# P V turned round in the attention of a fused audio tower, and the slot table emptied during the first attention

## The reference, cut to what matters

```python
content = einsum('bhld,bhmd->bhlm', q + u_bias, k)          # l = m = 345, h = 8, d = 64
pos_score = einsum('bhld,hmd->bhlm', q + v_bias, pos)
attn = softmax((content + pos_score) * 64 ** -0.5, axis=-1)
out = einsum('bhlm,bhmd->bhld', attn, v)                     # P V
out = transpose(out, (0, 2, 1, 3)).reshape(b, l, 512) @ w_out.T + b_out
...
xb = zeros((64, 256, 128)).at[flat_e, pos].set(x_rep, mode='drop')   # the slots
```

## Time and profile before

| what | value |
|---|---|
| three runs, us | 2994.98, 3003.32, 3011.47 |
| span of the profiled execution, us | 2993.0 |
| TensorE matmul busy | 2429.7 us, 81% |
| VectorE, ScalarE, GpSimd busy | 52%, 23%, 24% |
| first row out of the convolution (L1177) | 312.1 us |
| last L1177, start of the pass of batch 15 | 2526.8 us |

### The profile page before, as it was taken

How to read it: one execution, slowest core, us unless ns; L and a number is a source line. 1 busy time by engine, 2 the same in 40 slices (tenths; PEclk the granted TensorE clock), 3 DMA queues, 4 the chain that set the end, 5 groups by cost and what they waited for, 6 DMA issues and landing times. The chain is left out here.

```text
span 2993.0 us, 50876 instructions
## 1 busy us (share of the span) xinstructions
PE 2429.7 (81%) x17112; PEld 1799.3 (60%) x17112; DVE 1541.5 (52%) x4738; ACT 698.7 (23%) x1812; POOL 724.5 (24%) x610
## 2 busy tenths in 40 slices
PE   0503999999999999999999999999999999845661
PEld 0302676767676767676767676767677776633340
DVE  1210446565656465646474747474747464643441
ACT  1100222232323232313131313132323232302120
POOL 0000000303030304040404040404040404146886
PEclk9956999999999999999999999999999999967775
DMA  4700000101010101010000000000000000005674
GB/s 127 263 29 30 8 12 9 44 9 40 9 33 9 30 9 27 9 24 9 19 9 18 9 22 9 18 9 18 9 19 9 18 9 12 4 6 109 117 115 64
DMA packets 122647, 100.95 MB, mean 34 GB/s; under 512 B 60273, under 2 KB 116511, under 8 KB 121836
## 3 DMA queue, kind: packets, MB, share of 16 engines
q0 software_dynamic: 51904, 40.97, 7.1%
q1 hardware_dynamic: 68290, 54.06, 6.6%
q10 hardware_dynamic: 2200, 2.57, 0.3%
HBM read 71.57 MB, written 67.84 MB: 47 GB/s over the span
## 5 line engine op out<-in xcount | busy, mean ns | idle before, releaser
L641 PE MATMUL Cb<-y_hi,wc_hi 128*128 128x345 f16 x1984 | 623.1, 314 | 70.1 <-DVE zneg L1164 70.1
L641 PE MATMUL Cb<-y_hi,wc_lo 128*128 128x345 f16 x1984 | 622.0, 313 | 0.0
L641 PE MATMUL Cb<-y_lo,wc_hi 128*128 128x345 f16 x1984 | 621.3, 313 | 0.0
L569 POOL TENSOR_TENSOR rstd<-ve,minus_half 115x3 f32<-115x3 f32 x64 | 54.8, 857 | 1957.3 <-DVE ve L1201 1409.3
L581 POOL DMA_INDIRECT slots_dram<-rows,slot_i x384 | 452.3, 1178 | 133.8 <-issue 133.8
L1036 ACT ACTIVATE Pm<-W,nmax 115x345 f32<-115x345 f32 x384 | 211.2, 550 | 607.3 <-DVE nmax L1376 607.2
L641 PE MATMUL W<-x_hl,w_hl 128*128 128x345 f16 x1536 | 290.5, 315 | 32.3 <-DVE KP L1360 17.4
L641 PEld LDWEIGHTS Cb<-y_hi,wc_hi 128*128 128x128 f16 x1984 | 196.6, 99 | 192.5 <-DVE zneg L1164 70.4
L641 PE MATMUL W<-KP,qv 128*115 128x345 f32 x768 | 300.6, 473 | 0.8 <-issue 0.8
L641 PE MATMUL Ob<-qv,PT 115*115 115x64 f32 x2304 | 282.3, 259 | 17.8 <-DVE PT L1384 10.0
L641 PEld LDWEIGHTS Ob<-qv,PT 115*115 115x115 f32 x2304 | 263.4, 181 | 22.7 <-DVE PT L1384 12.1
(11 more groups left out here) (196 smaller groups left out, 2970.9 us busy)
## 6 DMA issues: line engine op xcount, KB each, us to landing
band<-band_dram SPq DMA_DIRECT2D x68, 182.1 KB
slots_dram<-in_empty_slots POOLq DMA_DIRECT2D x1, 12352.0 KB
wc_hi<-slots_dram SPq DMA_DIRECT2D x64, 193.0 KB
qv<-in_wc SPq DMA_DIRECT2D x8, 992.0 KB, 10.3
slots_dram<-rows,slot_i POOLq DMA_INDIRECT x384
x_win<-in_xpad SPq DMA_DIRECT2D x17, 248.0 KB
x_T<-in_xTp SPq DMA_DIRECT2D x17, 188.0 KB
band_dram<-lg SPq DMA_DIRECT2D x17, 182.1 KB
```

Of the source, the lines that this page charges most:

```text
L569: pool.tensor_tensor(rstd[g][:, :], ve[g][:, :], minus_half[:, :], ALU.pow)\
L641: return pe.matmul(o, l, r, start=start, stop=stop)
```

## The change

P V is turned round: V of a head (115x64) is the stationary operand and the transposed P (115x345) moves. Two heads are done together after the second one's last unit, the first into rows 0 to 63 of a bank `Ob`, the second into rows 64 to 127. The result is already transposed, so `O`, its 12 transposes and the copies are gone. As 1/sum now lies along the columns, TensorE spreads it over the rows ("N": six matmuls with the broadcast 1/sum stationary and the identity moving, a new use of the banks `W`), ScalarE copies it to `sums_b`, and VectorE multiplies. `PT` holds three heads. GpSimd empties the slot table in eight DMAs of 8 rows each during the attention of batch 0, each after three more units, and zeroes `odd_sum_dram` after the eighth; the loop over the batches begins once the table is empty.

```diff
 TOK_USE = ["lg"] + [x for t in range(TILES) for x in (f"bT{t}", f"y{t}")]
+PAIRS = H0 // 2
+PAIR_UNITS = 2 * J
+
+
+def pair_at(s, after):
+
+    p, r = divmod(s - after, PAIR_UNITS)
+    return p if r == PAIR_UNITS - 1 and 0 <= p < PAIRS else None
+
+
 def unit_steps():
     out = []
...
             out.append(("S", s))
         if 1 <= s <= UNITS:
             out.append(("T", s - 1))
+        if pair_at(s, 2) is not None:
+            out.append(("N", pair_at(s, 2)))
     return out
 W_USES = ([("ln", 1)] + [x for h in range(H0) for x in ([("q", h)] + ([("k", h // 2)] if h % 2 == 0 else []))]
           + [("v", j) for j in range(J)] + unit_steps()
-          + [("oT", j) for j in range(J)] + [("out0", 0)]
+          + [("out0", 0)]
           + [("ln", 2), ("gate0", 0)] + [("hid", n) for n in range(2 * E0)]
           + [("sg", 0), ("su", 0), ("sg", 1), ("su", 1)])
-O_USES = [("O", h) for h in range(H0)] + [("Y", e) for e in range(E0 + 1)]
+O_USES = [("O", p) for p in range(PAIRS)] + [("Y", e) for e in range(E0 + 1)]
 C_USES = [("conv", o) for o in range(OC)] + [("w2", 0)]
...
         psums = sb("psums", [A, H0, J])
         prec = sb("prec", [A, H0, J])
         Pm = sb("Pm", [A, 2, TOK])
-        PT = sb("PT", [A, 2, TOK])
+        PT = sb("PT", [A, 3, J, TOK])
+        sums_b = sb("sums_b", [128, TOK])
         k1 = sb("k1", [A, 3 * C])
         v1 = sb("v1", [A, 3 * C])
         tri_f = Pm[:, 0, :].rearrange("p (m a) -> p m a", m=3)
-        O = sb("O", [A, J, H0 * DH])
         hid = sb("hid", [128, 4, TOK])
         hidf = hid[:, :, :].rearrange("p j n -> p (j n)")
-        OT = hidf.rearrange("p (j n) -> p j n", j=J)
+        OT = hid
         peT, wposT = hidf[:, 0:TOK], hidf[:, TOK:TOK + H0 * DH]
         h1 = sb("h1", [A, J * C])
...
         def pt_used(eng, b, u):
+            h = u // J - 3
+            if h >= 0:
+                bank, nth = O_AT[("O", h // 2)]
+                eng.wait_ge(o_full[bank].h, o_full[bank].at(b, nth))
+
+        def pt_of(u):
+
             h, j = u // J, u % J
-            if j == J - 1:
-                bank, nth = O_AT[("O", h)]
-                eng.wait_ge(o_full[bank].h, o_full[bank].at(b, nth))
-            else:
-                eng.wait_ge(pv_done.h, pv_done.at(b, 2 * h + j + 1))
+            return PT[:, h % 3, :, j * A:(j + 1) * A]
         xpad, xTp = dram["xpad"], dram["xTp"]
...
                 pool.dma_start(ap(dst), src).then_inc(sig.h, 16)
             pool.dma_start(out[NTOK:, :], dram["empty_slots"][:, 0:C]).then_inc(h3_stored.h, 16)
-            pool.wait_ge(s_lo, 2 * OC)
-            pool.dma_start(slots_d.rearrange("(e s) n -> e (s n)", e=E1),
-                           dram["empty_slots"].rearrange("s n -> (s n)").unsqueeze(0).to_broadcast((E1, CAP * ROW)))\
-                .then_inc(rows_sent.h, 16)
-            pool.dma_start(odd_d.rearrange("(r s) c -> r (s c)", s=CAP),
-                           dram["zero_rows"].unsqueeze(0).to_broadcast((sum_rows // CAP, CAP * C))).then_inc(t_sum, 16)
+            def empty_slots(n):
+
+                first = n * (E1 // FILLS)
+                ins = pool.dma_start(slots_d.rearrange("(e s) n -> e (s n)", e=E1)[first:first + E1 // FILLS, :],
+                                     dram["empty_slots"].rearrange("s n -> (s n)").unsqueeze(0)
+                                     .to_broadcast((E1 // FILLS, CAP * ROW)))
+                if n < FILLS - 1:
+                    ins.then_inc(s_fill, 16)
+                else:
+                    ins.then_inc(rows_sent.h, 16)
+
+            def zero_sums():
+                pool.dma_start(odd_d.rearrange("(r s) c -> r (s c)", s=CAP),
+                               dram["zero_rows"].unsqueeze(0).to_broadcast((sum_rows // CAP, CAP * C))).then_inc(t_sum, 16)
             def hold():
                 if lb is not None:
                     send(lb)
-            present(0, None)
-
+            power(0, 1, 0)
+            for n in range(FILLS):
+
+                pool.wait_ge(p_ready.h, p_ready.at(0, (n + 1) * UNITS // FILLS))
+                empty_slots(n)
+            zero_sums()
+            power(0, 2, 0)
+
+            pool.wait_ge(s_fill, 16 * (FILLS - 1))
             pool.wait_ge(rows_sent.h, 16)
             pool.wait_ge(h3_stored.h, 16)
             with pool.Fori(1, B - 1) as it:
                         last = pe.transpose(w[0:A, i * A:(i + 1) * A], Pm[:, u % 2, i * A:(i + 1) * A], ident[0:A, 0:A])
                     return last
+                def spread_sums(w, g):
+                    for j in range(J):
+                        for r in range(2):
+                            last = mm(w[r * DH:(r + 1) * DH, j * A:(j + 1) * A],
+                                      prec[:, 2 * g + r, j:j + 1].to_broadcast((A, DH)), ident[0:A, 0:A])
+                    return last
+
                 for s in range(UNITS + 2):
                     if s < UNITS:
                         h, j = s // J, s % J
                         u = s - 1
                         pe.wait_ge(p_ready.h, p_ready.at(b, u + 1))
                         step(b, ("T", u), lambda w: turn_p(w, u))
-                    if s >= 2:
+                    g = pair_at(s, 2)
+                    if g is not None:
                         u = s - 2
-                        h, j = u // J, u % J
-                        if j == 0:
-                            o, was, nth = freed(("O", h))
-                            if was:
-                                pe.wait_ge(was.h, was.at(b, nth))
-                        pe.wait_ge((pt_ready_a, pt_ready_d)[u % 2].h, (pt_ready_a, pt_ready_d)[u % 2].at(b, u // 2 + 1))
+                        o, was, nth = freed(("O", g))
+                        if was:
+                            pe.wait_ge(was.h, was.at(b, nth))
+                        for v in u - 1, u:
+                            ready = (pt_ready_a, pt_ready_d)[v % 2]
+                            pe.wait_ge(ready.h, ready.at(b, v // 2 + 1))
                         for i in range(J):
-                            last = mm(Ob[o][0:A, j * DH:(j + 1) * DH], PT[:, u % 2, i * A:(i + 1) * A],
-                                      V[:, i, h * DH:(h + 1) * DH], start=(i == 0), stop=(i == J - 1))
-                        pv = o_full[o] if j == J - 1 else pv_done
-                        last.then_inc(pv.h, pv.up())
+                            for r in range(2):
+                                h = 2 * g + r
+                                last = mm(Ob[o][r * DH:(r + 1) * DH, 0:TOK], V[:, i, h * DH:(h + 1) * DH],
+                                          PT[:, h % 3, i, :], start=(i == 0), stop=(i == J - 1))
+                        last.then_inc(o_full[o].h, o_full[o].up())
+
+                        pe.wait_ge(prec_ready.h, prec_ready.at(b, g + 1))
+                        step(b, ("N", g), lambda w: spread_sums(w, g))
                 p = 3 + UNITS
                 conv(nb, p)
-                pe.wait_ge(o_ready.h, o_ready.at(b, H0))
-                for j in range(J):
-                    i, was, nth = freed(("oT", j))
-                    if was:
-                        pe.wait_ge(was.h, was.at(b, nth))
-                    for c in range(4):
-                        last = pe.transpose(W[i][:, c * A:(c + 1) * A], O[:, j, c * 128:(c + 1) * 128], ident[0:A, 0:A])
-                    last.then_inc(w_full[i].h, w_full[i].up())
                 conv(nb, p + 1)
                 i, was, nth = freed(("out0", 0))
                 if was:
                     pe.wait_ge(was.h, was.at(b, nth))
+                pe.wait_ge(o_ready.h, o_ready.at(b, PAIRS))
                 for j in range(J):
-                    pe.wait_ge(oT_ready.h, oT_ready.at(b, j + 1))
                     for c in range(4):
-                        last = mm(W[i][0:A, j * C:(j + 1) * C], OT[:, j, c * A:(c + 1) * A], woT[:, c, :],
+                        last = mm(W[i][0:A, j * C:(j + 1) * C], OT[:, c, j * A:(j + 1) * A], woT[:, c, :],
                                   start=(c == 0), stop=(c == 3))
                 last.then_inc(w_full[i].h, w_full[i].up())
...
                                                   accum_out=psums[:, s // J, s % J:s % J + 1]).then_inc(p_ready.h, p_ready.up())
                         late(lb, s)
                         conv_out(nb, 3 + s)
-                    if s >= 1 and (s - 1) % 2 == 0:
+                    if 1 <= s <= UNITS and (s - 1) % 2 == 0:
                         u = s - 1
                         i, nth = W_AT[("T", u)]
                         act.wait_ge(w_full[i].h, w_full[i].at(b, nth))
-                        if u >= 2:
-                            pt_used(act, b, u - 2)
-                        act.activation(PT[:, 0, :], W[i][0:A, 0:TOK], ACT.Copy).then_inc(pt_ready_a.h, pt_ready_a.up())
-                for j in range(J):
-                    i, nth = W_AT[("oT", j)]
-                    act.wait_ge(w_full[i].h, w_full[i].at(b, nth))
```

(50 more changed lines are left out.)

## The result

The changed kernel takes 3011.65 us (median of 19 runs, 3009.99 to 3017.85); the kernel before, run beside it, 3003.96 us. The ratio is 1.0032, with a 95% interval of 1.002 to 1.0044: slower by a third of a per cent. I had forecast 2957 us, 46 us faster; it lies 2 us above the upper end of my range. The span of the profiled execution went from 2993.0 to 3008.3 us.

The account below looks back on a forecast made before the run. TensorE was taken to bound the batch passes, behind an idle start. Span 2993.0 - 134 (start) + 83 (zeroing) + 5 (attention) = 2947 us, plus 10.3 for the median of runs: 2957 us, range 2865 to 3010.

Parts of the forecast that it names:

- What bounds the kernel: Whole kernel: TensorE is the bound in the batch passes and mostly idle for some 300 us before them.
- The start: Before batch 0's attention: with both GpSimd DMAs gone, weights land at 119 us and the start gains 134 us (120 to 136).
- The slot table: Batch 0's attention: eight DMAs of 8 rows, 8 to 14 us each if on half the engines, cost nothing.
- The zeroing: Batch 0's experts: moved, it lands some 114 us after the last exponential; TensorE waits 80 us for the band, 83 given back.
- Rival B: Batch 0's experts: the zeroing does not hold the band, by another engine or several packets a turn; 2879 us, chance 0.18.
- P V turned: Attention of all batches: less TensorE work but new waits, +0.7 us a full pass, about -1 in batch 0, +5 in all.
- TensorE's own work: Attention, per batch: 13.4 + 1.2 us removed, 10.8 added at 2.7 a pair, so 3.8 us less.
- Rival E: P V in the attention: the two column halves do not overlap, +154 us; slower than before at 3110 us, chance 0.10.
- The waits for N's bank: Attention: scores two units on wait 0.85 us for ScalarE's copy, three times a batch, 2.5 us.
- The middle waits: Attention, units 15 to 18: shorter units leave VectorE's stretches less slack, 1.3 us of new waiting.
- The tail: End of a batch's attention: the last pair's P V cannot start before VectorE's last copy, 0.7 us.
- Rival D: Attention: as in the 2957 us forecast, but uneven units cost VectorE's stretches more, 3 us a pass; 3005 us, chance 0.08.

Follow-up runs that it names:

- The run with 368 rows: Changed kernel with odd_sum zeroed by one DMA of 368 rows of 8 KB instead of 23 rows of 128 KB: 2930.7 us.
- the run with the attention alone: Changed kernel with GpSimd's DMAs put back as in the kernel before, leaving the turned P V and spread 1/sum: 3062.7 us, ratio 1.019 to the kernel before.
- the copy first: Changed kernel with ScalarE's copy to sums_b moved to the head of its step, before the exponential: 2985.3 us, ratio 0.9933 to the kernel before.
- the old P V and the mended DMAs: Kernel before, P V unchanged, with the slot fills moved as in the change and odd_sum zeroed in 368 rows of 8 KB: 2877.9 us, ratio 0.9568.

## Why the prediction was wrong

**What bounds the kernel** was right: the time moved where TensorE's idle time moved, at the start, in batch 0 and in the passes.

**The start** was right: 136.9 us instead of 134. The weights were there at 112.3 us (119 forecast, 113 at best), h0 of batch 0 at 175.2 (178).

**The slot table** was right: 10.5 us a DMA (8 to 14), and nothing waits for it.

**The zeroing** was right in mechanism and size: landed 119.7 us after its issue (114), one small packet for each large one, 82.3 us of TensorE's wait (80). It alone explains why so large a gain at the start left so little: 84 of 137 us went back to it, at a place the change made new. Rival B (another engine, or several packets at a turn) did not come. The run with 368 rows shows it was never a price of the move, only of 23 rows.

**P V turned** is where it failed, by four terms.

TensorE's own work was right. P V and N take 2.49 us a pair where I had 2.7, so 4 x 2.49 = 10.0 replace 14.6 us, -4.6 a pass (-3.8 forecast). Rival E (no overlap) is out, at 1.80 us for 12 records.

The waits for N's bank I had at 2.5 us; they are 0.46 + 0.43 + 0.68 = 1.6. The mechanism holds (it went with the copy's place), the size was too high: the fillers of those units are longer than the five that I took.

The middle waits, units 15 to 18, are 0.51 and 1.55 us against 0.19 before: 1.9 where I had 1.3.

The tail is the first step that failed. I gave it 0.7 us, for P V that cannot start before VectorE's last copy. It is 1.81 + 2.11 = 3.9 us against 0.64 + 0.51 + 0.71 = 1.9, so 2.1 more. VectorE's timeline of batch 3 shows what I left out:

```profile
787.88 0.52 DVE L1415 TENSOR_REDUCE nmax<-W 115x1 f32<-115x345 f32 x1 [0.21 <-DVE pos L1381]
788.31 0.57 DVE L1201 TENSOR_SCALAR z<-Cb,conv_b 128x345 f32<-128x345 f32 x1
...
791.12 0.52 DVE L1422 COPY PT<-W 115x345 f32<-115x345 f32 x1
```

The last row maximum stands behind the work on the expert counts, so the last exponential and transposes are late. The copy of that last transposed P, ready to be made at 789.7 us, stands behind the convolution's output and the choice of slots, until 791.12. Before, P V of unit 21 stood between the last two transposes and P V of unit 22 ahead of the last one, and they filled part of this. That VectorE's order makes these waits is read from the timeline; no run moved its work. I had looked at VectorE's row maxima only at units 16 and 17, and not at the last units.

The clock is the second, and it is a term that my sum for the attention put at nothing without a reason, though the start had one (2 to 3 us for a clock that had fallen in the wait). In batch 3 P V takes 1.67 us more, N 0.64 and the next convolution matmuls 0.7, 3.0 us in all. Where it falls for 3.4 us only, it is half of that: from this P V to the output projection the fourteen passes take 6.65 to 8.18 us, 7.46 in the mean, and 5.14 at the full clock (batch 0 of the run with the attention alone). So it costs 2.3 us a pass, less some 0.85 (half of 3.4 us lost, in every other pass) that the kernel before had too: +1.5.

The windows over batches 1 to 14, of before and of after (length, then TensorE's busy time):

```profile
448.71:2526.76 2078.05, 1967.69 (x14351) 1476.96 (x14351) 1232.24 (x3836) 549.38 (x1456) 452.48 (x406) 0.99 0.07 17
```

```profile
398.84:2533.70 2134.86, 1936.49 (x13511) 1347.45 (x13511) 1208.10 (x3724) 547.54 (x1470) 450.01 (x406) 0.98 0.06 16
```

TensorE's idle time in a pass rose by 6.3 us (7.9 to 14.2), of which these waits are 5.6. Together: -4.6 + 6.3 + 1.5 = +3.2 of the measured 4.1; 0.9 us a pass is not placed.

Two sums of the prediction do not come out either. Its +0.7 in fourteen passes less 1 in batch 0 is 9 us and not 5. And doubled waits are 9.0 us less 3.8, 5.2 a pass or some 73 us, where it says +45.

**Batch 15**, which I did not cost, has no convolution to fill any gap. From its h0 to its h1, windows of before and of after:

```profile
2526.70:2604.20 77.50, 63.03 (x409) 46.78 (x407) 51.30 (x171) 25.72 (x72) 2.58 (x3) 0.91 0.00 1
```

```profile
2533.70:2621.60 87.90, 62.18 (x348) 37.94 (x346) 49.81 (x163) 25.53 (x73) 2.58 (x3) 0.88 0.00 1
```

TensorE's busy time is 0.9 us less and its idle time 11.3 us more (25.7 against 14.5). The three waits for N's bank are 3.7 us of it, and with the copy first 3.4 us of the 10.4 came back. The rest, waits for exponentials and for PT, is read from the trace and was not tested; some of it may be the clock, since with the old P V and the mended DMAs this stretch took 81.8 us.

**Rival D** (3 us more a pass, 3005 us) was the nearest: it had a right place, VectorE's stretches, and with its 3.7 us a pass nine tenths of the 4.1. Part of that is luck, since the clock is not in it. With 0.08 it had too little: I took four unknown terms of the attention at their middle values and gave each no room above, while even my own figure for doubled waits was +45 us.

## What to carry to other kernels

A saving of work on a bound engine is worth only what is left after its gaps: work that came in small pieces, one to a unit, was also the filler of each unit's wait, and gathering it into one piece per pair opened gaps at every late neighbour. Look for the places where the engines around it are latest, the end of the loop first, and where the clock falls at a gap add its price: here 2.3 us a pass at waits of 3.9 us. And a DMA that is moved brings its shape along: 23 rows on one engine held up the small transfers beside them in the start and, once moved, in batch 0's experts too; before moving such a DMA, spread it.

## What the runs showed of the hardware

Twelve matmuls of 345 columns that alternate between the two halves of the columns take 1.80 us, where one after the other at the scores' 0.31 would be 3.7: the halves overlap fully. In head order they still overlap in part, also with the different matmuls that follow (0.63 us a pair lost and not the 1.3 that I expected).

The granted clock fell to half at waits of 1.8 and 2.1 us that lay 2.7 us apart, in all of fourteen passes. With only the 2.1 us ahead of P V it fell in 7, with only the 1.8 us ahead of the transposes in 9, and with only 2.1 us ahead of the transposes, 0.4 us a unit earlier, in 14. With waits of 0.4, 0.6 and 0.9 us it fell in none, but the 0.6, 0.5 and 0.7 us of the old P V brought it down in 7, 11 and 10 passes of fourteen in three kernels, and the 2.2 us at the start of the attention in 1 to 8. So no length of a single wait found here tells whether it falls.

A DMA of 66 KB packets on one engine let one small packet pass for each of its own, 12 for 12, in two places of two kernels. The Trainium skill (DMA: Bandwidth & Descriptors, "Queues, rings and completion order") has an engine drain some 9 to 17 descriptors of a ring before it turns to the next; here 12 small packets of some 2 KB passed in 28 us, so the measurement decides: one for one, and a stall of 82 us.
